# Graph layers on one Trainium2 core: one mixing matmul group per turn of 16 edge tiles in place of two of 8, with VectorE's one-hots made a turn ahead

## Chip, cores and metric

The kernel runs on 1 core of one Trainium2 chip. The metric is the device time of one execution in microseconds (us); less is better. An engine is named as the profile names it: PE is TensorE (PEld its weight loads), DVE is VectorE, ACT is ScalarE, POOL is GpSimd, SP is SyncE.

## What is computed

Four graph blocks run over 6,250 nodes with 128 features and one list of 106,250 edges, sorted by destination. Each block ends in a residual add and a layer norm. The blocks hold seven layers: five relational ones and two mean ones.

```python
# relational layer (three in block 0, two in block 2)
agg = segment_sum(h[src] @ W[etype], dst)        # 8 relations, W[r] is 128 x 128
h = relu(agg + h @ loopw + bias)  (+ h)
# mean layer (blocks 1 and 3)
agg = segment_sum(x[src] * weight, dst) / degree
x = concat(x, agg) @ W.T + b
```

The change touches the relational layers alone.

## The kernel before

**Tiles and turns.** The edges stand in 832 tiles of 128. The destinations of a tile lie in a window of 16 nodes, whose start is read at run time. A turn (`turn`, `messages`, `evacuate`) handles 16 tiles (`RING`), in two halves h of 8 (`HALF`), each half in two quarters q of 4 tiles. There are 52 turns in a layer (`TURNS`), so 260 in the five relational layers, which the trace shows from 18.7 to 1264 us, 1305 to 2596, 2629 to 3907, 4555 to 5824 and 5854 to 7120.

**What each engine does for one turn.**
- POOL (line 649) gathers the source rows of each tile from HBM by an indirect DMA, 8 per half, into `rows_in`. Before half h of a turn it waits for `summed[2h+1]` of the turn before (line 643), since the 8 places of that half are then free. Each place is written once a turn.
- DVE `onehots` (line 1300) makes the one-hot selectors of a quarter: 128 edges by 128 keys (16 nodes times 8 relations) for 4 tiles, as one instruction of 512 elements. It may overwrite them once `summed[2h+1]` has come.
- PE `messages` (line 1069) multiplies the gathered rows of a tile by its one-hot into a 128x128 piece of a PSUM bank, `SUM[q % 2]`, four tiles a bank. The last matmul of a quarter counts up `summed[q]`. It waits for the one-hots, for the four gathers one by one, and for the bank (`evacuated[(q + 2) % 4]`).
- ACT `evacuate_half` (line 777) copies the bank to `sums` in SBUF, sorted by relation, and counts up `evacuated[q]`. It waits for `summed[q]` and, ahead of each half, for `messaged[h]` of the turn before, since the mix has then read `sums`.
- PE (line 1082) mixes half h: 8 relations, each a 128x128 weight times 128 columns (8 tiles times 16 nodes), added up in its half of the PSUM bank `MIXED` (`MSG[h]`). The last one counts up `messaged[h]`. Ahead of the mix it waits for both evacuations of the half and for `added[7]` of the adds of that half's last use.
- DVE `adds` (line 1316) adds the 8 pieces of 128x16 to the columns of `acc` that their windows name, in order, each behind the one before by the semaphore `added[s]`.

A float32 matmul stands in the trace as two PE records, so a mix of a half is 16 records and a quarter of sums is 8.

**Order in a turn.** PE: sums of quarters 0 and 1, mix of half 0, sums of 2 and 3, mix of half 1. DVE (`turn`, line 1479): one-hots of half 1, adds of half 0, one-hots of half 0 of the turn that follows, adds of half 1. `opened` makes the one-hots of half 0 before the first turn. The engines' instruction streams are written out by hand in this order and each runs strictly in it.

**Fills.** In the four relational layers after the first, each half turn also builds four pieces of a dense adjacency matrix for the mean layers. DVE `hots` (lines 1396, 1400, 1405) makes markers into buffers of their own for each half, PE `fill` (line 955) multiplies them into two banks in turn, ACT `keep_fill` (line 748) copies them out and ACT's queue stores them by DMA (line 751). PE places the four fills of a half with `between`: two behind the sums of its quarters, one in the middle of its mix, one behind it. The fills are float32 in layers 1 and 2 and bfloat16 in layers 4 and 5.

**Steps between turns.** `edge_chunks` puts a step per chunk of 512 nodes between turns, once the adds for its nodes are done: DVE `columns` takes the chunk out of `acc`, PE turns it, ACT writes its rows to the table that the next layer gathers from. SP waits for `messaged` before each mean layer.

```python
pool.wait_ge(summed[2 * h + 1], k + (i + 1))                 # 643
pe.wait_ge(onehot_ready[q], this)                            # 1064
pe.wait_ge(evacuated[(q + 2) % 4], this)                     # 1065
pe.wait_ge(gathered[4 * q + t], landed)                      # 1067
pe.wait_ge(evacuated[2 * h + 1], following if h else this)   # 1077
pe.wait_ge(added[HALF - 1], taken[h])                        # 1078
act.wait_ge(messaged[h], k + 1)                              # 774
dve.wait_ge(summed[2 * h + 1], k + 1)                        # 1297
```

## Time and profile before

| what | us |
|---|---|
| runs shown | 7642.33, 7645.65, 7635.47 (median 7642.33) |
| the profiled execution | 7644.6 |
| its span in the profile | 7642.8 |
| busy: PE / PEld | 4968.5 / 4243.9 |
| busy: DVE / ACT / POOL | 3913.3 / 1543.1 / 3955.9 |
| idle before POOL's gathers from the tables | 2672.3 |
| granted share of PE's clock, mean | 0.797 |

The profiled execution's own time and its span differ by 1.8 us. Busy times are shares of an average over stages of different kinds: the five relational layers take some 6,350 us of the span, the rest are the two mean layers (3907 to 4555 and from 7120) and the short gaps between layers. Starts of PE instructions are recorded; their ends are modelled.

### The profile page before, as it was taken

Reading aid. Unit: us, or ns where it says so; the run is one execution under the profiler, and the core shown is the slowest. Engines: PE = TensorE matmul, PEld = TensorE weight load, DVE = VectorE, ACT = ScalarE, POOL = GpSimd, SP = SyncE. Lnnn points to the kernel's source line nnn. Section 1 sums busy time; section 2 is a strip of 40 time slices with the busy share of each in tenths; the row PEclk is TensorE's granted clock in tenths of the full one; section 3 lists DMA queues with packets and bytes.
Section 4 is the critical chain, followed back from the end, with each engine's and each line's share of the span. In section 5 each row is a group of like instructions: output and inputs, shape, how many; then the busy total and the mean of one; then the engine's idle time right before and its main releaser. Section 6 shows DMA issues by size and latency. Waiting matters only on the chain.

```text
span 7642.8 us, 106073 instructions
## 1 busy us (share of the span) xinstructions
PE 4968.5 (65%) x26408; PEld 4243.9 (56%) x26409; DVE 3913.3 (51%) x10762; ACT 1543.1 (20%) x3108; POOL 3955.9 (52%) x4190
## 2 busy tenths in 40 slices
PE   4444555667666667677679985555555555555799
PEld 4444444666666666666655545555554555555455
DVE  3222223555555555666666654444444454555666
ACT  1111111222222222222210012222222222222101
POOL 5666665566566566666630006666665666666100
PEclk7777766777878877878789997777777777777899
DMA  3122222344444334434458853333333333333464
GB/s 79 49 53 56 56 56 66 104 109 111 109 108 110 104 105 108 108 106 107 107 173 285 281 181 76 78 78 78 77 78 73 75 76 75 76 75 75 130 181 148
DMA packets 695057, 799.40 MB, mean 105 GB/s; under 512 B 307814, under 2 KB 582485, under 8 KB 694597
## 3 DMA queue, kind: packets, MB, share of 16 engines
q0 software_dynamic: 133952, 275.45, 17.5%
q10 hardware_dynamic: 481717, 270.72, 11.9%
q1 hardware_dynamic: 79184, 250.97, 10.1%
q8 instruction: 72, 1.18, 0.1%
q14 instruction: 132, 1.08, 0.0%
HBM read 529.43 MB, written 277.57 MB: 106 GB/s over the span
## 4 chain that ended last, share of the span: by engine, by line
PE 43%; another core or an unknown queue 28%; issue 15%; ACT 7%; ACTq 5%; DVE 2%; DMA 0%; DVEq 0%; SPq 0%
PE mixed L1082 17%; PE sum L986 6%; PE agg L955 5%; PE sum L1069 4%; ACT bulk L777 4%; PE fill L955 3%; ACT bulk L748 3%; PE mixed L986 3%; PE fill L986 3%; ACTq L751 2%; ACTq L161 1%; PE lin L930 1%; ACTq L154 1%; PE iota_ps L1112 1%
## 5 line engine op out<-in xcount | busy, mean ns | idle before, releaser
L649 POOL DMA_INDIRECT bulk<-h_table,srcT_i x3328 | 3151.9, 947 | 2672.3 <-remote 994.5
L1316 DVE TENSOR_TENSOR acc<-mixed,acc 128x16 f32 x4160 | 729.5, 175 | 2956.9 <-issue 1145.8
L1082 PE MATMUL mixed<-bulk,mix_w 128*128 128x128 f32 x4992 | 1092.2, 396 | 1277.7 <-ACT bulk L777 971.4
L1082 PEld LDWEIGHTS mixed<-bulk,mix_w 128*128 128x128 f32 x4992 | 1020.6, 300 | 1362.8 <-issue 1216.7
L1082 PE MATMUL mixed<-bulk,rel_w 128*128 128x128 f32 x3328 | 805.2, 420 | 1092.6 <-ACT bulk L777 1084.3
L1082 PEld LDWEIGHTS mixed<-bulk,rel_w 128*128 128x128 f32 x3328 | 722.6, 319 | 1143.3 <-issue 1138.2
L1069 PE MATMUL sum<-bulk 128*128 128x128 f32 x8320 | 1210.5, 295 | 23.8 <-issue 12.7
L1069 PEld LDWEIGHTS sum<-bulk 128*128 128x128 f32 x8320 | 1155.6, 213 | 35.0 <-issue 22.3
L777 ACT ACTIVATE bulk<-sum 128x512 f32<-128x512 f32 x1040 | 618.7, 598 | 2518.0 <-remote 1893.5
L649 POOL DMA_INDIRECT bulk<-in_x_dram,srcT_i x832 | 789.2, 949 | 482.0 <-issue 246.6
L1300 DVE TENSOR_TENSOR bulk<-iota_ps,keyT 128x512 f32<-128x512 f32 x1040 | 670.2, 686 | 210.6 <-issue 172.9
L1396 DVE TENSOR_TENSOR bulk<-iota_ps,low_key 128x392 bf16<-128x392 f32 (+1 forms) x1248 | 694.0, 556 | 5.1 <-issue 4.6
L748 ACT ACTIVATE bulk<-agg 128x392 f32<-128x392 f32 (+1 forms) x832 | 412.7, 496 | 1334.1 <-PE agg L955 835.6
L748 ACT ACTIVATE bulk<-fill 128x392 f32<-128x392 f32 (+1 forms) x832 | 417.8, 502 | 887.8 <-issue 355.6
L1400 DVE TENSOR_SCALAR bulk<-iota_ps,row_key,weight_of 128x128 f32<-128x128 f32 x1456 | 524.8, 402 | 1.8 <-issue 1.8
L986 PE MATMUL sum<-bulk,hT 128*128 128x448 f32 (+1 forms) x1176 | 434.9, 484 | 15.2 <-issue 7.8
L955 PE MATMUL agg<-bulk 128*128 128x196 f32 (+1 forms) x1664 | 419.7, 368 | 14.3 <-ACT bulk L748 8.0
L1432 DVE TENSOR_TENSOR bulk<-bulk 128x1792 f32<-128x1792 f32 (+1 forms) x192 | 344.1, 1792 | 103.3 <-DMA bulk<-adjacency_w 86.5
L955 PE MATMUL fill<-bulk 128*128 128x196 f32 (+1 forms) x1664 | 357.1, 322 | 27.9 <-issue 17.2
L1405 DVE TENSOR_TENSOR bulk<-iota_ps,row_key 128x256 bf16<-128x256 f32 x832 | 345.6, 415 | 3.9 <-issue 1.7
L955 PEld LDWEIGHTS agg<-bulk 128*128 128x128 f32 (+1 forms) x1664 | 292.7, 193 | 30.9 <-issue 14.6
L986 PEld LDWEIGHTS sum<-bulk,hT 128*128 128x128 f32 (+1 forms) x1176 | 187.1, 161 | 199.1 <-issue 163.8
(237 smaller groups left out, 3717.1 us busy)
## 6 DMA issues: line engine op xcount, KB each, us to landing
adjacency_w<-bulk ACTq DMA_DIRECT2D x416, 392.0 KB
bulk<-adjacency_w SPq DMA_DIRECT2D x147, 896.0 KB, 4.6
adjacency_n<-bulk ACTq DMA_DIRECT2D x416, 196.0 KB
bulk<-adjacency_n SPq DMA_DIRECT2D x147, 448.0 KB, 4.0
bulk<-h_table,srcT_i POOLq DMA_INDIRECT x3328
bulk<-adjacency_w SPq DMA_DIRECT2D x49, 448.0 KB, 4.1
bulk<-in_x_dram,srcT_i POOLq DMA_INDIRECT x832
h_table<-rows ACTq DMA_DIRECT2D x50, 256.0 KB
```

What stands on the lines that cost most here:

```text
L649: nc.gpsimd.indirect_dma_start(out=rows_in[:, s, :], out_offset=None, in_=rows_of[:, :], in_offset=bass.IndirectOffsetOnAxis(ap=srcT_i[:, ...
L748: act.activation(staged[m][s][:, f % 2 * 2 * LOWS:(f % 2 + 1) * 2 * LOWS], FILL[f % 2][:, 0:2 * LOWS], ACT.Copy).then_inc(fill_kept, 1)
L777: act.activation(sums[:, h, :, 4 * (q % 2):4 * (q % 2) + 4, :].rearrange("p r t v -> p t r v"), SUM[q % 2][:, :].rearrange("p (t r v) -> p ...
L955: last = nc.tensor.matmul(FILL[f % 2][:, w * LOWS:(w + 1) * LOWS], row[:, w, :], of[:, w, :], start=True, stop=True)
L986: last = nc.tensor.matmul(DENSE[s][:, 0:PIECE], x_k, (a_in, n_in)[m][t % bufs][:, s * PIECE:(s + 1) * PIECE], start=(n == 0 and k == 0), s ...
L1069: last = nc.tensor.matmul(SUM[q % 2][:, t * KEYS:(t + 1) * KEYS], rows_in[:, 4 * q + t, :], onehot[:, 4 * q + t, :], start=True, stop=True)
L1082: last = nc.tensor.matmul(MSG[h][:, 0:HALF * WIN], W[:, n, :], sums[:, h, n, :, :].rearrange("p t v -> p (t v)"), start=(n == 0), stop=(n ...
L1300: nc.vector.tensor_tensor(onehot[:, 4 * q:4 * q + 4, :], IOTA[:, 0:KEYS].unsqueeze(1).broadcast_to(each), keyT[:, bass.ds(i * RING + 4 * q ...
L1316: nc.vector.tensor_tensor(acc[:, at], MSG[h][:, s * WIN:(s + 1) * WIN], acc[:, at], ALU.add).then_inc(added[s], 1)
L1396: nc.vector.tensor_tensor(low_hots[f] if weighted else low_marks[f], IOTA[:, KEYS:NATURAL].unsqueeze(1).broadcast_to(each), low_key[:, bas ...
L1400: ins = nc.vector.tensor_scalar(row_hots[f][:, n, :], IOTA[:, NATURAL:NATURAL + D], row_key[:, bass.ds(w + n, 1)], weight_of[:, bass.ds(w ...
L1405: ins = nc.vector.tensor_tensor(row_marks[f], IOTA[:, NATURAL:NATURAL + D].unsqueeze(1).broadcast_to(each), row_key[:, bass.ds(w, 2)].unsq ...
```

## The change

Both halves of a turn are mixed by one group of 8 matmuls of 256 columns, behind the sums of all four quarters. `messaged` becomes one semaphore. PE waits once for evacuation (of quarter 3) and once for the adds of the turn before. DVE makes the one-hots of both halves of the following turn, and the fills' markers of both, and then adds all 16 pieces. `opened` makes both halves' one-hots. The fills of half 0 that stood in and behind its mix now stand between the sums of quarters 1 and 2; those of half 1 stand in and behind the one mix.

```diff
--- before.py
+++ after.py
@@ -379,7 +379,6 @@
 
         SUM = [bank("sum0"), bank("sum1")]
         MIXED = bank("mixed")
-        MSG = [MIXED[:, h * HALF * WIN:(h + 1) * HALF * WIN] for h in range(2)]
         LIN = [bank("lin0"), bank("lin1")]
         IOTA = bank("iota_ps")
         AGG = bank("agg")
@@ -402,7 +401,7 @@
         onehot_ready = [sem(f"onehot_ready{q}") for q in range(4)]
         summed = [sem(f"summed{q}") for q in range(4)]
         evacuated = [sem(f"evacuated{q}") for q in range(4)]
-        messaged = [sem(f"messaged{h}") for h in range(2)]
+        messaged = sem("messaged")
         added = [sem(f"added{s}") for s in range(HALF)]
         pass_moved = sem("pass_moved")
         waits_passed = sem("waits_passed")
@@ -547,9 +546,8 @@
                 m = layer["mean"]
                 if m == 0:
                     more_slices = slices_of(sp)
-                for h in range(2):
-                    sp.wait_ge(messaged[h], sp.snap(P * (REL_BEFORE[l] * TURNS) + 1))
-                    apart(sp)
+                sp.wait_ge(messaged, sp.snap(P * (REL_BEFORE[l] * TURNS) + 1))
+                apart(sp)
 
                 def restored():
                     if m == 0:
@@ -771,7 +769,8 @@
                         keep_lists(0)
 
                     def evacuate_half(h, k, between=None):
-                        act.wait_ge(messaged[h], k + 1)
+                        if h == 0:
+                            act.wait_ge(messaged, k + 1)
                         for q in (2 * h, 2 * h + 1):
                             act.wait_ge(summed[q], k + 1 + q % 2)
                             act.activation(
@@ -884,8 +883,7 @@
         def _(pe):
             for q in (1, 3):
                 pe.sem_inc(summed[q], 1)
-            for h in range(2):
-                pe.sem_inc(messaged[h], 1)
+            pe.sem_inc(messaged, 1)
             pe.sem_inc(filled, 8)
             pe.sem_inc(a_multiplied, A_BUFS)
             pe.sem_inc(degrees_turned, 1)
@@ -1059,7 +1057,7 @@
 
                         this, following = pe.snap(k + 1), pe.snap(k + 2)
                         landed = pe.snap(i * 16 + (GATHER_PASS * r + 16))
-                        taken = [pe.snap(k * 2 + (h + 2)) for h in range(2)]
+                        taken = pe.snap(k * 2 + 2)
                         for h in range(2):
                             for q in (2 * h, 2 * h + 1):
                                 pe.wait_ge(onehot_ready[q], this)
@@ -1071,20 +1069,23 @@
                                 last.then_inc(summed[q], 1)
                                 if between:
                                     between(h, q % 2)
-                            if h == 0 and layer["norm"] and c is not None and not (type(c) is int and c < 4):
-                                pe.wait_ge(x_kept, pe.snap(c + (NORM_BEFORE[l] * CHUNKS - 1)))
-                                apart(pe)
-                            pe.wait_ge(evacuated[2 * h + 1], following if h else this)
-                            pe.wait_ge(added[HALF - 1], taken[h])
-                            for n in range(N_RELS):
-                                if between and n == N_RELS // 2:
-                                    between(h, 2)
-                                last = nc.tensor.matmul(MSG[h][:, 0:HALF * WIN], W[:, n, :],
-                                                        sums[:, h, n, :, :].rearrange("p t v -> p (t v)"),
-                                                        start=(n == 0), stop=(n == N_RELS - 1))
-                            last.then_inc(messaged[h], 1)
-                            if between:
-                                between(h, 3)
+                            if between and h == 0:
+                                between(0, 2)
+                                between(0, 3)
+                        if layer["norm"] and c is not None and not (type(c) is int and c < 4):
+                            pe.wait_ge(x_kept, pe.snap(c + (NORM_BEFORE[l] * CHUNKS - 1)))
+                            apart(pe)
+                        pe.wait_ge(evacuated[3], following)
+                        pe.wait_ge(added[HALF - 1], taken)
+                        for n in range(N_RELS):
+                            if between and n == N_RELS // 2:
+                                between(1, 2)
+                            last = nc.tensor.matmul(MIXED[:, 0:RING * WIN], W[:, n, :],
+                                                    sums[:, :, n, :, :].rearrange("p h t v -> p h (t v)"),
+                                                    start=(n == 0), stop=(n == N_RELS - 1))
+                        last.then_inc(messaged, 1)
+                        if between:
+                            between(1, 3)
                 else:
                     pe.wait_ge(x_kept, 2 + CHUNKS * NORM_BEFORE[l])
                     pe.wait_ge(rows_ready, 4 + CHUNKS * l)
@@ -1301,20 +1302,21 @@
                                                 keyT[:, bass.ds(i * RING + 4 * q, 4)].unsqueeze(2).broadcast_to(each),
                                                 ALU.is_equal).then_inc(onehot_ready[q], 1)
 
-                def adds(h, i, k):
+                def adds(i, k):
                     _, starts = nc.values_load_multi_w_load_instructions(
-                        window[0:1, bass.ds(i * RING + HALF * h, HALF)], engines=[DVE], min_val=0, max_val=NP - WIN,
+                        window[0:1, bass.ds(i * RING, RING)], engines=[DVE], min_val=0, max_val=NP - WIN,
                         skip_runtime_bounds_check_because="starts are destinations, held to NP - WIN on the chip")
-                    earlier, this = dve.snap(k * 2 + (h + 2)), dve.snap(k * 2 + (h + 3))
-                    dve.wait_ge(messaged[h], k + 2)
-                    for s in range(HALF):
-                        if s:
-                            dve.wait_ge(added[s - 1], this)
+                    counts_of = [dve.snap(k * 2 + (h + 2)) for h in range(3)]
+                    dve.wait_ge(messaged, k + 2)
+                    for s in range(RING):
+                        h, place = s // HALF, s % HALF
+                        if place:
+                            dve.wait_ge(added[place - 1], counts_of[h + 1])
                         else:
-                            dve.wait_ge(added[HALF - 1], earlier)
+                            dve.wait_ge(added[HALF - 1], counts_of[h])
                         at = bass.ds(starts[s], WIN)
-                        nc.vector.tensor_tensor(acc[:, at], MSG[h][:, s * WIN:(s + 1) * WIN], acc[:, at],
-                                                ALU.add).then_inc(added[s], 1)
+                        nc.vector.tensor_tensor(acc[:, at], MIXED[:, s * WIN:(s + 1) * WIN], acc[:, at],
+                                                ALU.add).then_inc(added[place], 1)
 
                 def mark_steps():
 
@@ -1470,23 +1472,21 @@
 
                     def opened(p):
 
-                        onehots(0, 0, dve.snap(count(P, p, r, 0)))
-                        if layer["fills"] and p is more:
-                            fill_at(0, 0)
+                        for h in range(2):
+                            onehots(h, 0, dve.snap(count(P, p, r, 0)))
+                            if layer["fills"] and p is more:
+                                fill_at(0, h)
                         dve.wait_ge(acc_set, 2 + CHUNKS * (r + 1))
 
                     def turn(i, k, c=None, filling=False):
-                        onehots(1, i, k)
-                        if filling:
-                            fill_at(i, 1)
-                        adds(0, i, k)
                         with dve.If(i < TURNS - 1):
                             following = nc.s_assert_within(i + 1, min_val=1, max_val=TURNS - 1,
                                                            skip_runtime_bounds_check_because="the condition above")
-                            onehots(0, following, k + 1)
-                            if filling:
-                                fill_at(following, 0)
-                        adds(1, i, k)
+                            for h in range(2):
+                                onehots(h, following, k + 1)
+                                if filling:
+                                    fill_at(following, h)
+                        adds(i, k)
 
                     def turn_filling(i, k, c=None):
                         turn(i, k, c, True)
```

## Rows read from the trace of the kernel before

**Rows 1.** The page's parts 1 and 4: busy time, and the chain by engine.

```profile
PE 4968.5 (65%) x26408; PEld 4243.9 (56%) x26409; DVE 3913.3 (51%) x10762; ACT 1543.1 (20%) x3108; POOL 3955.9 (52%) x4190
...
PE 43%; another core or an unknown queue 28%; issue 15%; ACT 7%; ACTq 5%; DVE 2%; DMA 0%; DVEq 0%; SPq 0%
```

**Rows 2.** The five relational layers: length, busy PE, PEld, DVE, ACT, POOL, granted clock.

```profile
18.00:1264.00 1246.00, 618.00 (x3395) 581.69 (x3395) 303.05 (x1088) 140.77 (x241) 781.65 (x824) 0.73 0.22 55
1305.00:2595.00 1290.00, 878.56 (x4953) 844.02 (x4953) 747.49 (x2266) 309.50 (x642) 782.23 (x825) 0.79 0.40 107
2629.00:3907.00 1278.00, 896.07 (x4968) 847.13 (x4966) 773.90 (x2407) 308.94 (x646) 779.70 (x824) 0.80 0.40 106
4555.00:5824.00 1269.00, 706.75 (x4126) 656.75 (x4125) 611.50 (x1847) 326.11 (x641) 779.61 (x824) 0.76 0.36 77
5854.00:7119.00 1265.00, 707.53 (x4156) 655.70 (x4154) 636.69 (x1969) 325.75 (x647) 780.22 (x824) 0.77 0.36 75
```

**Rows 3.** Timeline, half a turn with float32 fills: start, busy us, instructions, idle before.

```profile
2112.09 0.60 ACT L777 ACTIVATE bulk<-sum 128x512 f32<-128x512 f32 x1 [2.46 <-remote]
...
2112.82 2.07 PE L1082 MATMUL mixed<-bulk,mix_w 128*128 128x128 f32 x8 [4.77 <-ACT bulk L777]
2112.86 0.95 POOL L649 DMA_INDIRECT bulk<-h_table,srcT_i  x1 [2.37 <-remote]
...
2114.68 1.51 PE L955 MATMUL agg<-bulk 128*128 128x196 f32 x4
...
2115.99 1.74 PE L1082 MATMUL mixed<-bulk,mix_w 128*128 128x128 f32 x8
...
2117.96 2.33 DVE L1316 TENSOR_TENSOR acc<-mixed,acc 128x16 f32 x8 [4.87 <-issue]
...
2118.23 1.05 PE L1069 MATMUL sum<-bulk 128*128 128x128 f32 x8
...
2119.78 1.05 PE L1069 MATMUL sum<-bulk 128*128 128x128 f32 x8
...
2121.62 0.95 POOL L649 DMA_INDIRECT bulk<-h_table,srcT_i  x1 [0.30 <-issue]
...
2124.29 0.60 ACT L777 ACTIVATE bulk<-sum 128x512 f32<-128x512 f32 x1 [5.35 <-remote]
...
2125.17 0.60 ACT L777 ACTIVATE bulk<-sum 128x512 f32<-128x512 f32 x1
2125.17 0.95 POOL L649 DMA_INDIRECT bulk<-h_table,srcT_i  x1 [2.60 <-remote]
```

**Rows 4.** Timeline, first layer, 16 gathers without a pause between the halves.

```profile
77.82 0.95 POOL L649 DMA_INDIRECT bulk<-in_x_dram,srcT_i  x1 [3.92 <-remote]
...
78.23 3.78 PE L1082 MATMUL mixed<-bulk,mix_w 128*128 128x128 f32 x16 [12.19 <-ACT bulk L777]
...
83.56 0.60 ACT L777 ACTIVATE bulk<-sum 128x512 f32<-128x512 f32 x1 [5.47 <-PE sum L1069]
...
86.06 0.60 ACT L777 ACTIVATE bulk<-sum 128x512 f32<-128x512 f32 x1 [1.90 <-remote]
...
87.82 0.94 POOL L649 DMA_INDIRECT bulk<-in_x_dram,srcT_i  x1 [0.30 <-issue]
...
90.14 1.95 PE L1069 MATMUL sum<-bulk 128*128 128x128 f32 x16
...
96.57 0.95 POOL L649 DMA_INDIRECT bulk<-in_x_dram,srcT_i  x1 [0.30 <-issue]
...
100.30 1.08 ACT L777 ACTIVATE bulk<-sum 128x512 f32<-128x512 f32 x2 [13.64 <-remote]
101.10 0.94 POOL L649 DMA_INDIRECT bulk<-in_x_dram,srcT_i  x1 [3.58 <-remote]
```

**Rows 5.** All instructions by line and shape: count, busy us, mean ns.

```profile
L1316 DVE TENSOR_TENSOR acc<-mixed,acc 128x16 f32 x4160 | 729.5, 175 | 2956.9 <-issue 1145.8 <-PE mixed L1082 943.3 <-remote 390.4
...
L1300 DVE TENSOR_TENSOR bulk<-iota_ps,keyT 128x512 f32<-128x512 f32 x1040 | 670.2, 686 | 210.6 <-issue 172.9 <-ACT weight_of L739 15.5 <-DVE window L1277 2.2
```

## The prediction

> **What bounds the kernel now.** I read the page first: PE is busy for 65% of the span, no engine for more, and 28% of the chain that ended last is time behind a releaser the profile can't name [rows 1]. So no engine is full, and a loop of waits is to be looked for. The five relational layers take 6,348 us of the span, and only they are changed. In them POOL issues 16 gathers a turn at the same pace whatever else is done: divided out (stretch / gathers x 16) a turn takes 24.2 us in the first layer and 25.1, 24.8, 24.6 and 24.6 in the others, although PE's busy time differs by 45% between them (618 to 896 us) and DVE's by 2.5 times [rows 2]. A loop whose length doesn't follow PE's or DVE's work is not set by them.
>
> The timeline of half a turn shows the loop [rows 3]. POOL starts its first gather at 2112.86 and its eighth at 2121.62, 8.76 us later (1.25 us each). The first of the next half starts at 2125.17, so 3.55 us behind the eighth, where 1.25 would be the pace: 2.3 us of pause. A half is thus 12.31 us, a turn 24.6. POOL waits there for the semaphore of the second quarter's sums. By the record those matmuls (those at 2119.78) were issued by 2120.8, but ACT, which waits for sums too, starts the copy of the first of these two quarters only at 2124.29 and of the second at 2125.17. So a semaphore of the sums is seen 3 to 5 us after its matmul, about when the gathers in flight can have landed; the mix's is seen at once (PE ends it near 2117.7, DVE adds from 2117.96). I can't say from these rows why. I take it as a fact: the sums' semaphores come late when PE reaches them late in a batch of eight gathers, and this delay, not PE's rate, makes the pause.
>
> The first layer shows the other case [rows 4]. There one quarter's copy starts at 83.56 and the other's at 86.06, before POOL has issued its batch out, and POOL goes from one half into the next without a pause (87.82 is 1.25 us behind its predecessor). The next release comes only behind the sixteenth gather (96.57): ACT at 100.30, POOL at 101.10. That turn took 101.10 - 77.82 = 23.28 us.
>
> **The change, part by part.**
>
> *The matmuls.* 16 records of 128 columns become 16 of 256 per turn instead of 32 of 128. The columns set this pace; the weight loads (PEld 844 us beside PE's 879 [rows 2]) lie under it. So a 256-column record should take twice as long and the mix saves nothing: 0 us. The bound on one side is half of the loads, if they did stand in the way: 4,160 fewer at 0.16 us (4243.9 / 26,409 [rows 1]), 670 us of PE's time, which would still not shorten a loop that PE doesn't set. The Trainium skill (Perfetto Trace Analysis, section Matmuls) says that larger matmuls are more efficient than smaller ones; by that rule PE's time would fall, by the rows above it stays, and the sum would be the same by both, since POOL's loop holds it.
>
> *One wait in place of two.* PE now issues all four quarters of sums of a turn, waits for the copy of quarter 3, mixes, and goes on with the sums of the next turn. Two things follow. The sums of quarters 2 and 3 stand directly behind the release of quarters 0 and 1, with no mix before them: copy 0.6 us, sums 1.0 to 1.7 us a quarter at either clock, so in the first layer they are out some 4 us after the release, in the layers with bfloat16 fills 5 to 6 us, with float32 fills 6 to 8 us. Today these sums stand behind 16 records of mix: in [rows 3] 6.9 us after PE's start. And a mix's semaphore, which today has that early place, is not held up. I take it that the semaphore of quarter 3 will then mostly be there when POOL has its eight gathers out (10.0 us), as at 86.06 in [rows 4], so POOL goes into the second half without a pause. The other half of the turn becomes heavier: a copy, a mix of 6.9 us at the lower level or 3.5 at the higher, two fills, the sums of quarters 0 and 1. Its release stays behind the last gather. A turn becomes that of [rows 4], 23.28 us.
>
> Price: 24.62 - 23.28 = 1.34 us a turn in four layers, x 208 = 279 us; in the first layer 24.2 - 23.28 = 0.9, x 52 = 47 us; 326 us in all. Bounds: 0 if the pause stays in both halves, 4.6 us a turn (24.6 - 20.0, 16 gathers at 1.25) if it goes from both. I take three quarters of 326, 245 us, nearest to the row of the same pattern, because in the float32 layers PE reaches quarter 3 late in a part of the turns.
>
> *DVE.* Adds and one-hots are as many as before: 16 x 0.29 = 4.7 us and 4 x 0.64 = 2.6 us a turn [rows 3, 5]. All DVE work of the heaviest layer is 774 us / 52 = 14.9 us a turn [rows 2], so 8 us and more are idle. New is that the adds are queued behind the one-hots and markers of both halves, and the markers of half 1 wait for fills that now stand in the mix. The adds will so come up to half a turn later. Who waits for them is PE's next mix, most of a turn on: cost 0, the idle 8 us are the cover; if that cover were gone, PE would wait, which is a rival below. The one-hots are made half a turn earlier than today or as early: 0.
>
> The Trainium skill (Perfetto Trace Analysis, section Matmuls) says that independent matmul groups should rotate through PSUM banks so that one's evacuation overlaps the next. This change goes the other way: before, the two halves had semaphores of their own; now one group can't start before all 16 adds of the last. By the rule that costs; no row of the kernel before has this wait.
>
> *ACT and POOL.* ACT's copies of quarters 0 and 1 wait for the one `messaged`, which is earlier in time than the sums they copy: 0. Fills: as many; ACT's copies of half 0's come closer together, and ACT is busy for a quarter of the time (309 of 1,290 us [rows 2]). POOL's gathers, its waits and its DMAs are the same. SP waits for `messaged` once instead of twice before two layers: 0, and its waits for `summed[3]` in the first layer only place background stores.
>
> *Ends of layers.* The last turn has nothing to hide the larger mix behind: 3.5 us more of mix, 8 x 0.29 = 2.3 us more of adds, and the first turn makes 1.3 us more of one-hots and, with fills, markers. About 6 us a layer, 30 us in all; bounds 0 and 60.
>
> **Sum.** 7644.6 (the profiled execution, 1.8 over its span, 2.3 above the median of the three runs) - 245 + 30 = 7429.6, and 2 less against the median: I say 7430.
>
> **Rivals.**
> *The loop stays locked* (chance 0.30). The pause remains in both halves, since the late semaphore is tied to the gathers in flight and not to PE's place. For it: the releases in [rows 3] come where the eighth gather can just have landed; in the layers with fills the delay is the same with heavy and with light work. Against: [rows 4]. Time: 7645 + 30 = 7675, between 7640 and 7700. I give 0.13 of it to within 0.2% and 0.17 to slower.
> *The heavy half becomes the bound* (0.17), slower. Place: from the release of quarter 3 to the last sum of the next turn's quarter 1, PE does a copy's wait of 0.7 us, 16 records of 256, three fills and 16 records of sums. At the lower level that is 0.7 + 6.9 + 3 x 1.4 + 3.4 = 15.2 us, at the higher about 8; allowed are 12.3 us less about 1, if the loop is locked. It decides from a mean of about 11 us on. Price: up to 3 us a turn in the 104 turns with float32 fills, 1 in the others: 100 to 400 us with the ends, 7,830 as a middle. For it: the granted clock is only 0.73 to 0.80 [rows 2]. Against: if the pause of one half goes, a turn leaves this chain over 20 us.
> *DVE's adds are exposed* (0.03): that rule's case. If the markers wait for the mix's fills and the adds behind them for PE, up to 4.7 us a turn would come onto the path, 7,800 to 8,800.
> *Both pauses go* (0.02): 20.0 us a turn, 7645 - 260 x 4.6 = 6,450.
> That the change doesn't do what it says has no place here: the instructions are counted in the diff; only its saving on PE is nil.
>
> **Numbers.** Forecast 0.48; its own range is 7,330 (all turns like [rows 4]) to 7,560 (a quarter of them). About 0.2% is what a measurement of this kernel can tell from no change (15 us). Faster: 0.48 + 0.02 = 0.50. Same: 0.13. Slower: 0.17 + 0.17 + 0.03 = 0.37. The range goes from 7,300 to 7,830: it leaves out half of the heavy-half case, the adds and the case of both pauses, and a little below.
>
> **What would show it.** In the changed kernel's timeline POOL's ninth gather of a turn 1.25 us behind its eighth, and one pause of 3 to 4 us a turn; 832 gathers in about 1,215 us in the float32 layers. `mixed` matmuls half as many, each twice as long, their busy time unchanged. DVE's adds in one run of 16. Wrong: two pauses a turn still (the locked loop); one pause much above 4 us, with PE busy up to the release (the heavy half); PE's idle time ahead of the mix put down to DVE's adds (the third). If PE's busy time in the mix falls by a third or more, my count of the weight loads is wrong.

## The result and the profile after

The changed kernel takes 7865.12 us (median of 3 runs, 7864.77 to 7875.04) against 7642.33: a ratio of 1.029, 95% interval 1.0275 to 1.0304. The forecast of 7430 us is wrong in sign, and the range of 7300 to 7830 does not hold the time. The profiled execution spans 7863.3 us, against 7642.8 before: 220.5 us are to be found.

The page of the changed kernel, parts 1 and 4, beside [rows 1]:

```profile
PE 4870.6 (62%) x22248; PEld 3787.7 (48%) x22249; DVE 3949.0 (50%) x10762; ACT 1538.1 (20%) x3108; POOL 3943.5 (50%) x4190
...
PE 36%; another core or an unknown queue 32%; issue 14%; ACT 6%; ACTq 4%; DVE 4%; POOL 2%; DMA 1%; DVEq 1%; POOLq 0%; SPq 0%
```

No engine is much busier than before (VectorE 36 us more, PE 98 and GpSimd 12 less); the share behind a releaser that the profile can't name rose from 28% to 32%. The five relational layers of the changed kernel (busy time by stretch, columns as in [rows 2]):

```profile
19.00:1244.00 1225.00, 632.22 (x2604) 508.85 (x2603) 304.57 (x1085) 141.21 (x243) 779.03 (x824) 0.67 0.22 56
1279.00:2582.00 1303.00, 832.63 (x4156) 736.79 (x4154) 768.66 (x2294) 321.63 (x653) 778.13 (x825) 0.83 0.39 106
2620.00:3973.00 1353.00, 839.97 (x4152) 742.80 (x4151) 784.44 (x2407) 320.64 (x647) 778.30 (x825) 0.82 0.37 100
4632.00:5944.00 1312.00, 696.20 (x3309) 566.68 (x3307) 617.05 (x1837) 315.15 (x642) 777.20 (x824) 0.71 0.33 74
5981.00:7327.00 1346.00, 707.46 (x3339) 577.56 (x3338) 643.40 (x1963) 317.05 (x646) 778.45 (x824) 0.71 0.32 70
```

Against [rows 2] the layers changed by -21, +13, +75, +43 and +81 us, 191 together; the other 29 us lie between the layers and behind the last, the term that the prediction called ends of layers and put at 30. They aren't the even 6 us a layer of the prediction: behind the five layers, in order, the changes are -6, +4, +11, +7 and +12 us (and +1 ahead of the first), so the agreement of the sum is in part luck. The table of waits by GpSimd (line, what it waited for: us in all, times, longest) says how, first of the kernel before:

```profile
POOL bulk L649 <- remote: 1200.5, 464, 4.2
...
POOL bulk L649 <- PE sum L1069: 106.5, 24, 16.1
```

and of the changed kernel:

```profile
POOL bulk L647 <- remote: 800.1, 316, 4.5
...
POOL bulk L647 <- PE sum L1067: 688.0, 110, 33.1
```

Of the half turns, 85, 103, 102, 101 and 102 began with a pause in the five layers before, and 51, 100, 96, 82 and 81 do now. But 110 of GpSimd's waits now last 6.3 us on average. To see which, I took for each turn the time from GpSimd's first gather to that of the next turn, 51 turns a layer:

| relational layer | turns up to 25.7 us, their mean | 25.7 to 28 us: number, us over 24.5 | over 28 us: number, us over 24.5 |
|---|---|---|---|
| before, 1 to 5 | 46 to 49; 23.60, 24.73, 24.75, 24.49, 24.50 | 3, 2, 2, 3, 2; 21 in all | 2, 1, 0, 0, 0; 20, 14, 0, 0, 0 |
| after, 1 | 49; 23.46 | 0 | 2; 17 |
| after, 2 | 47; 24.58 | 2; 5 | 2; 33 |
| after, 3 | 37; 24.53 | 6; 16 | 8; 74 |
| after, 4 | 23; 24.53 | 28; 52 | 0 |
| after, 5 | 28; 24.26 | 15; 28 | 8; 65 |

Three things stand in it: 16 very long turns in the third and fifth layer (139 us), turns of some 26.3 us, above all in the two bfloat16 layers (79 us more than before), and two turns of the second layer, mostly its first (19 us). What is left of the gain is the balance to 191, 46 us, of which 21 are the first layer's. The 19 us can't be put down to the change: one and the same kernel, run twice on one chip, showed that first turn at 50.5 us and at 33.3 (e10 and e16 below), where it is 52.9 here and 38.3 before.

**The first layer has the forecast pattern, but not its gain.** Timeline, one turn of the changed kernel:

```profile
703.84 0.95 POOL L647 DMA_INDIRECT bulk<-in_x_dram,srcT_i  x1 [0.30 <-issue]
...
713.84 0.94 POOL L647 DMA_INDIRECT bulk<-in_x_dram,srcT_i  x1 [0.30 <-issue]
717.64 1.09 ACT L776 ACTIVATE bulk<-sum 128x512 f32<-128x512 f32 x2 [18.28 <-remote]
...
718.47 0.94 POOL L647 DMA_INDIRECT bulk<-in_x_dram,srcT_i  x1 [3.69 <-remote]
```

The gathers left out start every 1.25 us, through the change of halves too (703.84 is the turn's eighth); from the start of the sixteenth gather to that of the next turn's first are 4.6 us (713.84 to 718.47), as in [rows 4]. The regular turns fell only from 23.60 to 23.46 us. By the starts of the gathers, the kernel before already had this pattern in 11 first-layer turns, at 23.66 us, beside 29 turns with both pauses, at 23.77: where the pause between the halves is missing, the one behind the sixteenth gather is longer (4.7 us in place of 3.0, from start to start).

**A very long turn.** Timeline of the changed kernel, third layer, where a chunk of nodes is finished:

```profile
3057.62 1.89 PE L1083 MATMUL mixed<-bulk,mix_w 128*128 128x256 f32 x8
...
3059.34 0.83 PE L953 MATMUL fill<-rel_w,bulk 128*128 128x196 f32 x4
...
3061.69 0.57 DVE L1398 TENSOR_TENSOR rel_w<-iota_ps,low_key 128x392 f32<-128x392 f32 x1 [2.56 <-PE fill L953]
3061.82 0.95 POOL L647 DMA_INDIRECT bulk<-h_table,srcT_i  x1 [0.30 <-issue]
...
3063.52 4.78 DVE L1318 TENSOR_TENSOR acc<-mixed,acc 128x16 f32 x16 [0.63 <-issue]
...
3068.45 1.09 PE L921 MATMUL mixed<-ident,rows 128*128 128x128 f32 x4 [7.84 <-DVE acc L1318]
...
3069.33 1.91 PE L1067 MATMUL sum<-bulk 128*128 128x128 f32 x8
...
3072.34 1.91 PE L1067 MATMUL sum<-bulk 128*128 128x128 f32 x8
...
3075.06 0.94 POOL L647 DMA_INDIRECT bulk<-h_table,srcT_i  x1 [12.30 <-PE sum L1067]
```

The same step of the kernel before:

```profile
3066.33 1.05 PE L1082 MATMUL mixed<-bulk,mix_w 128*128 128x128 f32 x8
...
3067.53 2.33 DVE L1316 TENSOR_TENSOR acc<-mixed,acc 128x16 f32 x8 [3.20 <-issue]
...
3070.01 0.63 PE L923 MATMUL mixed<-ident,rows 128*128 128x128 f32 x4 [1.52 <-issue]
...
3070.70 1.15 PE L1069 MATMUL sum<-bulk 128*128 128x128 f32 x8
3071.20 0.95 POOL L649 DMA_INDIRECT bulk<-h_table,srcT_i  x1 [0.30 <-issue]
...
3074.97 0.95 POOL L649 DMA_INDIRECT bulk<-h_table,srcT_i  x1 [2.82 <-PE sum L1069]
```

At the end of a chunk PE transposes normalised rows back (`back`, L921 after, L923 before) into the bank `mixed`, so it waits for every add out of that bank, and the next turn's sums stand behind it. Before, the last 8 adds start 0.15 us behind the mix, and `back` follows them 0.15 us on. After, VectorE has the next turn's markers of half 1 ahead of the adds; they wait for the fill behind the mix, so the adds start 4.0 us behind the mix (3059.51 to 3063.52), and there are 16 of them. GpSimd's pause, from start to start, is 13.24 us instead of 3.77. How long PE waited for VectorE's adds over the whole kernel (us in all, times, longest), ahead of the mix (L1082) and ahead of `back` (L923), before:

```profile
PE mixed L1082 <- DVE acc L1316: 118.5, 16, 12.0
...
PE mixed L923 <- DVE acc L1316: 12.3, 7, 2.0
```

and after, where the mix (L1083) has no such wait, with another wait that the change made:

```profile
PE agg L953 <- ACT bulk L746: 757.1, 203, 10.9
...
PE mixed L921 <- DVE acc L1318: 166.4, 19, 18.6
```

**A turn of 26 us.** The first of these lines (8.0 us, once, for the same wait before) is a second ring. Timeline of the changed kernel, fourth layer:

```profile
5210.92 0.44 PE L953 MATMUL agg<-bulk 128*128 128x196 bf16 x2
...
5213.55 1.06 PE L1067 MATMUL sum<-bulk 128*128 128x128 f32 x8
...
5216.12 0.94 POOL L647 DMA_INDIRECT bulk<-h_table,srcT_i  x1 [0.30 <-issue]
5219.43 0.50 ACT L746 ACTIVATE bulk<-agg 128x392 bf16<-128x392 f32 x1 [9.48 <-remote]
...
5220.07 0.48 PE L953 MATMUL agg<-bulk 128*128 128x196 bf16 x2 [5.46 <-ACT bulk L746]
5220.35 1.96 PE L1067 MATMUL sum<-bulk 128*128 128x128 f32 x8
...
5223.12 0.94 POOL L647 DMA_INDIRECT bulk<-h_table,srcT_i  x1 [6.05 <-PE sum L1067]
```

The fill in the mix is done at 5211.36, but ScalarE copies it out only at 5219.43, 3.3 us behind GpSimd's last gather. PE's first fill of the next turn needs that copy and stands between the sums of quarter 0 (5213.55) and quarter 1 (5220.35). GpSimd waits for quarter 1: 7.0 us from start to start in place of some 3.6.

### The profile page after: what moved, and what is told of

It reads as the page before. It is cut to its first block, busy times and chain, and to the rows that moved or that the text cites. A ratio compares the mean times of both kernels' runs of the same rounds, so it can differ in the third digit from the quotient of the medians.

```text
span 7863.3 us, 96647 instructions
## 1 busy us (share of the span) xinstructions
PE 4870.6 (62%) x22248; PEld 3787.7 (48%) x22249; DVE 3949.0 (50%) x10762; ACT 1538.1 (20%) x3108; POOL 3943.5 (50%) x4190
## 4 chain that ended last, share of the span: by engine, by line
PE 36%; another core or an unknown queue 32%; issue 14%; ACT 6%; ACTq 4%; DVE 4%; POOL 2%; DMA 1%; DVEq 1%; POOLq 0%; SPq 0%
PE mixed L1083 10%; PE sum L1067 6%; PE sum L984 6%; PE agg L953 4%; PE fill L953 3%; ACT bulk L746 3%; PE mixed L984 2%; PE fill L984 2%; ACT bulk L776 2%; ACTq L749 2%; POOL bulk L647 2%; DVE acc L1318 1%; ACTq L161 1%; DMA adjacency_n<-bulk 1%
## 5 line engine op out<-in xcount | busy, mean ns | idle before, releaser
L1067 PE MATMUL sum<-bulk 128*128 128x128 f32 x8320 | 1467.9, 331 | 546.3 <-ACT bulk L776 381.9
L1067 PEld LDWEIGHTS sum<-bulk 128*128 128x128 f32 x8320 | 1353.7, 241 | 608.8 <-issue 509.2
L1083 PE MATMUL mixed<-bulk,mix_w 128*128 128x256 f32 x2496 | 853.4, 506 | 653.4 <-ACT bulk L776 592.5
L1083 PEld LDWEIGHTS mixed<-bulk,mix_w 128*128 128x128 f32 x2496 | 634.1, 262 | 812.4 <-issue 697.8
L953 PE MATMUL agg<-bulk 128*128 128x196 f32 (+1 forms) x1664 | 394.9, 350 | 852.0 <-ACT bulk L746 757.1
L1083 PE MATMUL mixed<-bulk,rel_w 128*128 128x256 f32 x1664 | 598.1, 522 | 509.6 <-issue 314.8
L1083 PEld LDWEIGHTS mixed<-bulk,rel_w 128*128 128x128 f32 x1664 | 427.9, 271 | 614.2 <-issue 537.4
L953 PEld LDWEIGHTS agg<-bulk 128*128 128x128 f32 (+1 forms) x1664 | 238.5, 166 | 953.9 <-issue 934.7
L1398 DVE TENSOR_TENSOR rel_w<-iota_ps,low_key 128x392 f32<-128x392 f32 x416 | 233.4, 561 | 491.0 <-PE agg L953 151.0
L953 PE MATMUL fill<-bulk 128*128 128x196 f32 (+1 forms) x1664 | 379.4, 338 | 98.5 <-ACT bulk L746 59.6
```

The lines of the kernel that those rows point to most:

```text
L953: last = nc.tensor.matmul(FILL[f % 2][:, w * LOWS:(w + 1) * LOWS], row[:, w, :], of[:, w, :], start=True, stop=True)
L1067: last = nc.tensor.matmul(SUM[q % 2][:, t * KEYS:(t + 1) * KEYS], rows_in[:, 4 * q + t, :], onehot[:, 4 * q + t, :], start=True, stop=True)
L1083: last = nc.tensor.matmul(MIXED[:, 0:RING * WIN], W[:, n, :], sums[:, :, n, :, :].rearrange("p h t v -> p h (t v)"), start=(n == 0), stop= ...
L1398: nc.vector.tensor_tensor(low_hots[f] if weighted else low_marks[f], IOTA[:, KEYS:NATURAL].unsqueeze(1).broadcast_to(each), low_key[:, bas ...
```

## The experiments

Three theories were set against each other: the fill handshake just shown (T1), a heavy half in which the mix itself is too long (T2), and VectorE's new order (T3). An interval in brackets is 95%. Chips differ: the kernel before took 7648 us on the chip of e1 to e4, 7653 on that of e5 to e8, 7786 on that of e9 to e16, 7657 on the last. Each ratio is to the kernel before on the same chip. The drain at the chunks (T4) came up behind e1 to e4.

**e1**: PE's fills of half 0 behind quarter 1's sums.

```diff
-                                if between:
+                                if between and h:
                                     between(h, q % 2)
                             if between and h == 0:
-                                between(0, 2)
-                                between(0, 3)
+                                for f in range(4):
+                                    between(0, f)
```

> The changed kernel, with TensorE's four fills of half 0 issued behind the sums of quarter 1 instead of one of them between the sums of quarter 0 and quarter 1. The turns of the changed kernel take, layer by layer, 23.8, 25.3, 26.3, 25.5 and 26.1 us. Theory 1 (the fill handshake: this fill waits for ScalarE's copy of the last fill of the turn before, whose semaphore is seen only when the gathers in flight have landed, and the sums that GpSimd waits for stand behind it): the turns of the four layers with fills come towards the first layer's 23.8, 1.5 to 2.5 us less each, 208 turns, so 200 to 420 us less than 7865, 7450 to 7660. Theory 2 (the heavy half: TensorE has too much to do between quarter 3's release and quarter 1's sums, mostly the mix of 256 columns): only the one fill of 0.7 to 1.4 us leaves the way, at most 0 to 1 us a turn, 7650 to 7865, and TensorE is busy up to quarter 1's sums. Theory 3 (VectorE's adds or one-hots are late since they moved): no change, 7850 to 7880.

7712.8 us, 1.0083 (1.0065 to 1.0101). About 150 us less than the changed kernel: above T1's range, and inside the one I had given T2. What tells them apart is where it went. The turns of 25.7 to 28 us are all but gone (1 of 51 in the fourth layer, 0 in the fifth), and GpSimd's waits for sums fell by half:

```profile
POOL bulk L647 <- PE sum L1067: 307.6, 48, 30.5
```

The 16 turns over 28 us stayed (64 and 58 us over 24.5, from 74 and 65), and the two float32 layers still pause twice a turn, which T1 had not reckoned with. By T2 the 26 us turns would have lost the one fill of at most 1.4 us, and PE would be busy up to quarter 1's sums; they lost 1.8 us, and what stood there was a wait.

**e2**: both halves' fills behind both quarters' sums, ScalarE's copies of sums ahead of those of fills.

```diff
...
-                                if between:
-                                    between(h, q % 2)
-                            if between and h == 0:
-                                between(0, 2)
-                                between(0, 3)
+                            if between:
+                                for f in range(2 if h else 4):
+                                    between(h, f)
```

> The changed kernel, with the fills of each half behind the sums of both its quarters on TensorE, and ScalarE's copies of both quarters ahead of its copies of fills. Theory 1 (the fill handshake): no quarter's sums and no quarter's copy stand behind a fill now, so the layers with fills come at least as near to the first layer's 23.8 us a turn as with half 0 alone: 7430 to 7640. Theory 2 (heavy half, the mix's length): 7650 to 7865. Theory 3 (VectorE): 7850 to 7880.

7720.5 us, 1.0093 (1.0075 to 1.0111): nothing beyond e1, and again above T1's range.

**e3**: one mix, VectorE's order of before.

```diff
...
                     def turn(i, k, c=None, filling=False):
+                        onehots(1, i, k)
+                        if filling:
+                            fill_at(i, 1)
                         with dve.If(i < TURNS - 1):
...
-                            for h in range(2):
-                                onehots(h, following, k + 1)
-                                if filling:
-                                    fill_at(following, h)
+                            onehots(0, following, k + 1)
+                            if filling:
+                                fill_at(following, 0)
                         adds(i, k)
```

> The changed kernel with VectorE's order of one-hots and markers of before: those of half 1 at the start of the turn, those of the next turn's half 0 ahead of the adds; the one mix of 16 tiles and the one run of 16 adds stay. It undoes the part of the change that is VectorE's alone. Theory 3 (the new order on VectorE is what costs): towards the time before, 7640 to 7750. Theories 1 and 2 (the way runs through TensorE and ScalarE, VectorE's part costs nothing): 7840 to 7900, the light half's and the heavy half's lengths as in the changed kernel; a slower time than that would say that making one-hots a turn ahead helps.

7732.7 us, 1.0097 (1.0075 to 1.0119): T3's range, which I had counted as the weakest. The long turns shrink from 74 and 65 us over 24.5 to 42 and 36, the turns of 25.7 to 28 us from 100 us over 24.5 to 48 (with no fill moved), and what PE waited for adds ahead of `back` from 166.4 us to:

```profile
PE mixed L921 <- DVE acc L1318: 76.4, 13, 13.8
```

**e4**: e2's order of fills and copies in the kernel before.

```diff
...
                                 last.then_inc(summed[q], 1)
-                                if between:
-                                    between(h, q % 2)
+                            if between:
+                                for f in range(2):
+                                    between(h, f)
```

> The kernel before, with the fills of each half behind the sums of both its quarters (TensorE), and ScalarE's copies of both quarters ahead of its copies of fills. In the kernel before the turns are 24.2 us without fills and 24.6 to 25.0 with them. Theory 1 (the handshake costs only where a fill stands ahead of sums that are on the way): the layers with fills come to 24.2 or below, 0.4 to 0.9 us x 208 turns, 80 to 190 us less, 7450 to 7560. Theory 2 (TensorE's amount of work per half sets the half): the amount is the same, so 7620 to 7660. If the fills' new place makes the mix late instead: slower than 7660.

7618.1 us, 0.9959 (0.9944 to 0.9973): faster by 30 us, where T1 said 80 to 190. The fills' place costs little as long as two mixes leave no fill's copy on the way.

**e5 and e6**: `back` writes to `sum0`, in the changed kernel and in e1's. PE's wait for `x_kept`, ScalarE's copy of what `back` wrote, moves with it from ahead of the mix to the start of the turn.

```diff
-        BACK = {REL: MIXED, MEAN: AGG}
+        BACK = {REL: SUM[0], MEAN: AGG}
...
-                    pe.wait_ge(added[HALF - 1], pe.snap(taken))
+                    pe.wait_ge(evacuated[2], pe.snap(taken))
```

> The changed kernel, with the transposes back of a finished chunk (PE's function back) written to the bank sum0 in place of the bank mixed, so that they wait for ScalarE's copy of quarter 2 and no longer for the 16 adds out of mixed. In the changed kernel eight turns of the third relational layer take 33 to 34 us where their neighbours take 24.5, and eight of the fifth 29 to 35; each of them follows the end of a chunk, where PE waits for all adds before it transposes back, and the next sums stand behind it. Theory 4 (these turns are the drain: one mix and 16 adds must end before the bank is free): they fall to about the neighbours, 16 turns x 6 to 9 us, and some turns behind them with 27.5 too, 100 to 180 us less than 7865: 7690 to 7765. Rival (the drain comes from the chunk's other work, columns and normalising behind the adds on VectorE): 7830 to 7880.

> The changed kernel with both remedies: the four fills of half 0 behind the sums of quarter 1, and the transposes back in the bank sum0. The first alone measured 7713. If the handshake of the fills and the drain at the chunks are separate costs, both gains add: 7713 less 90 to 160, 7550 to 7625, below the kernel before (7642). If they are one cost seen twice: 7690 to 7720.

e5: 7847.6 us, 1.0242 (1.0225 to 1.026); e6: 7687.3 us, 1.0037 (1.0023 to 1.0051). Both miss, e5 by far; e6 comes out 3 us under its second range. The wait mostly moved. `back` now runs at once (3045.46 in e6), but the next sums need ScalarE's copy out of `sum0`, and ScalarE stands behind the late fill. Timeline of e6:

```profile
3045.46 0.60 PE L921 MATMUL sum<-ident,rows 128*128 128x128 f32 x4
...
3047.27 0.50 ACT L746 ACTIVATE bulk<-fill 128x392 f32<-128x392 f32 x1 [3.94 <-remote]
...
3051.27 0.58 ACT L707 ACTIVATE xT<-sum 128x512 f32 x1
...
3052.35 3.78 PE L1070 MATMUL sum<-bulk 128*128 128x128 f32 x16 [6.29 <-ACT xT L707]
```

So the bank alone is not the cause. It has a part in it: e6 lies below e1 (1.0037 against 1.0083, on two chips), and its long turns hold 91 us over 24.5 where e1's hold 123.

**e7 and e8**: GpSimd waits quarter by quarter, in the kernel before and in e4's.

```diff
-                        for h in range(2):
-                            pool.wait_ge(summed[2 * h + 1], k + (i + 1))
+                        for q in range(4):
+                            pool.wait_ge(summed[q], k + (i + 1))
...
```

> The kernel before, with GpSimd waiting for the sums quarter by quarter (summed 0 ahead of four gathers, summed 1 ahead of the next four) instead of for the second quarter of a half ahead of all eight. Theory A (the semaphores of both quarters' sums come at about the landing of the last gather in flight, the first some 0.9 us ahead of the second): each half starts up to 0.9 us earlier, 520 halves, of which I count a half to all: 230 to 450 us less, 7190 to 7410. Theory B (TensorE's chain of sums and mix sets the period and the pause only shows it): the gathers start earlier and wait later, 7620 to 7660.

> The kernel before with the waits of GpSimd quarter by quarter and the fills of a half behind both quarters' sums (the two edits of e4 and e7 together). In e4 the fills' new place alone measured 0.996 of before. Theory A: both gains, 7160 to 7390, as the first quarter's semaphore comes at the landing but the second's now has no fill ahead of it. Theory B: 7600 to 7640, as e4.

7666.4 us, 1.0018 (1.0007 to 1.0029), and 7670.4 us, 1.0022 (1.0011 to 1.0034): theory A falls, as a forecast of the time, and for e8 even theory B was too good. The trace of e7 shows more than its time. Its regular turns are shorter in the four layers with fills (24.46, 24.63, 24.20 and 24.22 us, before 24.73, 24.75, 24.49 and 24.50), but nine turns in the third and fifth layers now take some 30 us and hold 49 us over 24.5. An earlier start of four gathers buys a little in every turn, and as much is lost in these, with two mixes and VectorE's order of before.

**e9**: one mix in the first and fourth relational layer alone, two elsewhere, on e4's base.

```diff
+        ONE_MIX = (0, 4)
...
+                        one = l in ONE_MIX
                         for h in range(2):
...
+                            if one:
+                                continue
                             if h == 0 and layer["norm"] and c is not None
...
+                        if one:
...
+                                last = nc.tensor.matmul(MIXED[:, 0:RING * WIN], W[:, n, :],
```

> The one mix of 16 tiles, with VectorE's order and adds of the change, in the first and the fourth relational layer only (those that have no chunks to normalise and, by their gathers, gained or can gain: 1,225 against 1,246 us in the first, 1,248 against 1,268 in the fourth once the fills stand behind the sums); the other three keep two mixes of 8 tiles. Fills stand behind both quarters' sums everywhere, as in e4 (7618). If the mix's cost is the handshake of the fills and the drain at the chunks, neither of which these two layers now have: 7618 less 20 to 45, 7570 to 7600, the first kernel here clearly below the one before. If a mix of 16 costs by itself (TensorE's heavy half): 7620 to 7680.

7756.9 us, 0.9962 (0.9948 to 0.9976), on a chip on which the kernel before is slower; as a gain over e4 (0.9959 elsewhere) it shows none. By layer it is less clear. Against e12, which has the instructions of the kernel before on this chip, the two layers with one mix are 24 and 15 us shorter (1241.3 and 1268.6 us from the first gather to the last half's; 1265.5 and 1284.0), and the third layer, with two mixes, is 14 longer: seven of its turns take some 32 us, where e12 has four. Whether the new place of the fills makes these, no run on this chip shows.

**e10 and e16**: e1 and e3 together. It was run twice, both times on the slow chip, although the text of e16 speaks of another.

> The changed kernel with the fills of half 0 behind the sums of quarter 1 (e1, 7713) and with VectorE's order of before (e3, 7733); only the one mix and the one run of 16 adds are left of the change. If both edits remove the same wait (the fills' handshake; VectorE's markers for half 1's fills are a link of it): 7690 to 7720, no better than the better one. If they remove different ones (the fills on TensorE's way, VectorE's queue ahead of the adds at the chunks): the gains add in part, 7610 to 7680.

> The same kernel as e10: one mix, fills of half 0 behind quarter 1's sums, VectorE's order of before. Measured on another chip: 0.994. If the two remedies add: 0.990 to 1.003 and at least 0.005 below e14. If the gain was that chip's: as e14, 1.005 to 1.012.

7738.1 us, 0.9937 (0.992 to 0.9953), and 7731.3 us, 0.9931 (0.9913 to 0.9949). The first was expected as a time of the faster chips, and is comparable only as a ratio: there it is below e1 and e3, though on another chip.

**e11 and e15**: VectorE's order alone, two mixes. It too was run twice, both times on the slow chip, so e15 can't tell whether the cost is that chip's. The markers of half 1 stand between the two runs of adds, since PE's second mix needs the first run.

```diff
-                        onehots(1, i, k)
-                        if filling:
-                            fill_at(i, 1)
-                        adds(0, i, k)
                         with dve.If(i < TURNS - 1):
...
                                 fill_at(following, 0)
+                            onehots(1, following, k + 1)
+                        adds(0, i, k)
+                        with dve.If(i < TURNS - 1):
...
+                            if filling:
+                                fill_at(following, 1)
                         adds(1, i, k)
```

> The kernel before with two mixes of 8 tiles, and VectorE's one-hots of both halves made a turn ahead of their use, as in the change; the markers of half 1 stand between the two runs of 8 adds, as far ahead as two mixes allow. It does the change's VectorE part alone. If the new order costs by itself: 7700 to 7780, as e3 gave back 130 us. If it costs only with one mix, whose 16 adds stand behind it: 7635 to 7665. If one-hots made early help: below 7635.

> The same kernel as e11: two mixes, VectorE's one-hots of both halves a turn ahead. Measured on another chip: 1.021. Theory V (the order is the larger cost because the adds stand behind one-hots that wait for the sums of the running turn): 1.015 to 1.025 again. If the first result was that chip's: 1.00 to 1.01.

7950.2 us, 1.0207 (1.0187 to 1.0227), and 7950.4 us, 1.0214 (1.0196 to 1.0232). With e13 and e14 on the same chip the change comes apart:

> The changed kernel as it is, beside e14, e15 and e16 on one chip, since times of one kernel differ by some 2% between chips. Measured first: 1.029 of before. Expected 1.015 to 1.035.

> The same kernel as e3: the one mix and the run of 16 adds, VectorE's one-hots and markers in the order of before. With e11 (VectorE's order alone) and the changed kernel this makes the four combinations. Measured as e3: 1.010. If VectorE's order is the larger cost, this stays at 1.00 to 1.012, and e15 above it; if the one mix is the larger, this lies above 1.015.

| same chip | ratio | us over 24.5 in turns over 28, layers 3 and 5 |
|---|---|---|
| one mix alone (e14) | 0.9969 (0.9956 to 0.9982) | 42, 29 |
| VectorE's order alone (e15) | 1.0214 (1.0196 to 1.0232) | 75, 68 |
| both, the change (e13) | 1.0113 (1.0095 to 1.0131) | 82, 65 |
| one mix, fills behind sums (e16) | 0.9931 (0.9913 to 0.9949) | 38, 20 |

VectorE's order by itself is worse than the whole change and makes the same long turns. Its 165 us are not its price in the change, though. With two mixes it also puts the adds of half 0 behind one-hots that wait for quarter 3's sums, which with one mix stand ahead of the adds anyway. In the change the order costs 113 us on this chip (e13 less e14). Timeline of e15, the end of a chunk:

```profile
3162.04 0.57 DVE L1396 TENSOR_TENSOR rel_w<-iota_ps,low_key 128x392 f32<-128x392 f32 x1 [3.20 <-remote]
...
3163.25 2.33 DVE L1316 TENSOR_TENSOR acc<-mixed,acc 128x16 f32 x8
...
3165.73 1.08 PE L923 MATMUL mixed<-ident,rows 128*128 128x128 f32 x4 [5.01 <-DVE acc L1316]
...
3171.74 0.94 POOL L649 DMA_INDIRECT bulk<-h_table,srcT_i  x1 [11.74 <-PE sum L1069]
```

The same chain as in the changed kernel, with two mixes: a marker that waits, adds behind it, `back` behind them. Its other turns in the layers with fills are longer too, 25.0 to 25.3 us, but only a little: e12, the instructions of before on this chip, has 24.9 to 25.1. e13 and e14 came out lower than I had written; the one mix alone is a small gain on this chip and a loss of 1% on that of e3, and e16 lies 0.4% below it, not the 0.5% asked for, though by both its runs below the kernel before. The fills' place is worth less here because the 26 us turns are nearly absent: in e13, the changed kernel itself, the turns of 25.7 to 28 us hold 36 us over 24.5, in e12 29, where they hold 100 and 21 in the first profiles of the two kernels. Yet PE's fills wait for ScalarE about as often and as long in e13 as in the first profile (300 times, 738 us, against 288 times, 817 us), so that row alone doesn't tell what the ring costs.

**e12**: sums of the identity matrix instead of the gathered rows.

```diff
-                                    last = nc.tensor.matmul(SUM[q % 2][:, t * KEYS:(t + 1) * KEYS], rows_in[:, 4 * q + t, :],
+                                    last = nc.tensor.matmul(SUM[q % 2][:, t * KEYS:(t + 1) * KEYS], ident[:, :],
```

> The kernel before, with the sums taken of the identity matrix in place of the gathered rows; TensorE still waits for each gather. It leaves out the messages' data, nothing of the instructions. If TensorE's sums are seen late because it reads the memory that the gathers write to: the pause of 3.6 us a half goes or shrinks, 6500 to 7400. If the lateness is one of the semaphores and the gathers in flight: 7630 to 7660, same pauses.

Measured once: 7795.2 us against 7785.8 before on that chip, with the pauses as they were (2.90 us):

```profile
2173.77 0.94 POOL L649 DMA_INDIRECT bulk<-h_table,srcT_i  x1 [0.31 <-issue]
2177.61 0.94 POOL L649 DMA_INDIRECT bulk<-h_table,srcT_i  x1 [2.90 <-remote]
```

That PE reads what the gathers write is not why its semaphores are late.

**e17**: e16 with the 16 adds ahead of the next turn's markers of half 0; **e18**: the kernel before.

```diff
                             onehots(0, following, k + 1)
-                            if filling:
-                                fill_at(following, 0)
                         adds(i, k)
+                        if filling:
...
+                                fill_at(following, 0)
```

> The kernel of e10 and e16 (one mix, the fills of half 0 behind quarter 1's sums, VectorE's order of before) with one more edit: VectorE's run of 16 adds stands ahead of the next turn's markers of half 0, not behind them. Sixteen turns behind the ends of chunks still take 28 to 30 us in e16 where their neighbours take 24.8, about 60 us in all. If VectorE's queue (markers that wait for fills, adds behind them) makes these turns long: 30 to 60 us less than e16, 0.985 to 0.990 of before where e16 was 0.993. If it is ScalarE's and TensorE's work at the chunk: as e16, within 10 us. If markers made later hold up the fills: slower than e16.

> The kernel before itself, for its profile on a second chip, as its times differ between the chips (about 7650 and 7785) while those of the changed kernel don't (7865 and 7871). If the difference sits in the turns at the ends of chunks: eight turns of the third relational layer at 31 to 33 us on the slower chip, as in e12's trace, none on the faster. If it sits in every turn: 24.9 to 25.1 us instead of 24.5 to 24.8, with the landing of a gather 0.2 us later. On the same chip as the first time: as before, 7633 to 7655.

e17 takes 7716.3 us, 1.0082 (1.0061 to 1.0103), and its long turns are still 27 to 35 us: a miss. These markers were not the rest of the drain. Whether e16 itself would be faster than before on this chip is open: it was run on the slow one alone, and e17 differs from it by chip and edit at once. Its time is 15 us below e16's, its ratio 1.5% above. e18 is the kernel before (0.9988) on a chip like the first. There it has two such long turns in the third layer (16 us over 24.5) and none in the fifth; e12, the same instructions on the slow chip, has four there (34 us), not the eight of e18's text. So the kernel before has some of these long turns too. That a chip's timing decides how many is argued, not shown: GpSimd's idle time behind the eighth gather is 2.9 us there (median, e12) and 2.7 here. No run profiles the kernel before itself, with the gathered rows, on the slow chip.

## Why the prediction was wrong

From the forecast to the time are 435 us: 199 of gain that did not come, 139 for the long turns at the ends of chunks, 79 for the turns of 26 us and 19 in the second layer, mostly its first turn.

**The first release without a pause** (the gain of 245 us): right in place in the first layer, far too large in size. The first layer gave 21 of the 47 us counted at full; the five layers together 46. The term mis-sized is the price of a pause, 1.34 us a turn, which set a turn of one layer against turns of others. In one layer, turns without the second pause are shorter than those with it by 0.1 us in the kernel before (first layer, 23.66 against 23.77), and by 0.6 and 0.8 us in the bfloat16 layers of e1: what one pause loses, the other takes up in part. The 24.2 us for the first layer was a stretch divided out, and two turns of 35 and 33 us were in it; its regular turns took 23.60 already, 0.3 above [rows 4]. The step "I take it that the semaphore of quarter 3 will then mostly be there when POOL has its eight gathers out" held in one layer and failed in the two with float32 fills, which still pause in 100 and 96 of 103 half turns (103 and 102 before); in the bfloat16 layers it held in about a fifth (82 and 81 pauses, 101 and 102 before). Timeline of the changed kernel, second layer:

```profile
2131.05 1.05 PE L1067 MATMUL sum<-bulk 128*128 128x128 f32 x8
...
2135.91 0.94 POOL L647 DMA_INDIRECT bulk<-h_table,srcT_i  x1 [0.30 <-issue]
...
2138.64 0.60 ACT L776 ACTIVATE bulk<-sum 128x512 f32<-128x512 f32 x1 [1.01 <-remote]
...
2139.41 0.94 POOL L647 DMA_INDIRECT bulk<-h_table,srcT_i  x1 [2.56 <-remote]
```

PE reaches quarter 3 almost 5 us ahead of the eighth gather, as I had worked out, and its semaphore comes behind that gather all the same. I had generalised from a layer without fills ([rows 4]) to layers with them. That is the locked loop (0.30) for these layers; its price of 30 us for the ends of layers is what was measured in all (29), with a different split.

**The adds queued behind one-hots and markers, "cost 0"**: the largest cost that the sum put at nothing. I wrote that the adds come up to half a turn later and that only PE's next mix waits for them. `back` waits for them as well, and so does VectorE's own reading of a finished chunk; both stand in the loop at every end of a chunk, sixteen times in two layers, at 5 to 11 us each. The rival had the right mechanism, markers that wait for the fills in the mix and the adds behind them, but I charged it to every turn, gave it 7,800 to 8,800 and a chance of 0.03. The time fell in that interval at its low end. Without VectorE's new order the change takes 132 us less than where it was first timed (e3, 1.0097 in place of 1.029) and 113 us less on the slow chip (e14, 0.9969 in place of 1.0113). Only on the slow chip does that turn the sign. On chips like the first every kernel with one mix in all layers is slower than the kernel before, by 0.4 to 2.9%: the gain that should have carried the change was too small to pay for anything. And the order is not the whole of the long turns. Of the 139 us in them, e3 keeps 79; the one mix with its 16 adds makes these by itself (e14: 71 us, e12 34).

The rule of the Trainium skill (Perfetto Trace Analysis, section Matmuls), that matmul groups should rotate through PSUM banks, was set aside because "no row of the kernel before has this wait". That reading was wrong: PE's mix waited for the adds 16 times before, 118.5 us in all, 15 of them in the first layer; one of 9.8 us ends at 101.9, just behind the turn of [rows 4]. After the change the mix has none of these waits, so what the prediction feared did not happen at the mix. The wait shows ahead of `back`, the bank's other writer, at 166.4 us, so the trace agrees that a shared bank is where a wait shows; e5 and e6, with the bank changed, won little of it.

**"Fills: as many; copies come closer together", 0**: wrong. The fill in the mix is copied late, and the first fill of the next turn stood between quarters 0 and 1. It is 79 us in the table. e1 leaves 6 of the 100 us that these turns hold, and e3, with no fill moved, leaves 48, so VectorE's order feeds this ring as well, and the gains of e1 and e3 don't simply add.

**The heavy half** (0.17) named the right half and the right sign, near the right time, for the wrong reason: PE was not busy up to the release, it stood for 5.46 us on ScalarE's copy. e1, which shortens no mix, shows that.

**The mix saves nothing on PE**: nearly right. Its busy time fell from 1897.4 us (1092.2 + 805.2) to 1451.5:

```profile
L1083 PE MATMUL mixed<-bulk,mix_w 128*128 128x256 f32 x2496 | 853.4, 506 | 653.4 <-ACT bulk L776 592.5
...
L1083 PE MATMUL mixed<-bulk,rel_w 128*128 128x256 f32 x1664 | 598.1, 522 | 509.6 <-issue 314.8
```

Eight records of 256 columns take 3.77 us at 1.2 GHz and 1.89 at 2.4 (granted clock 0.50 and 1.00 in the two parts of the mix at 3053 and 3057.6), sixteen of 128 take 3.78 us at 1.2 GHz in [rows 4]: the same columns, the same time. In the trace the records of 128 columns start 0.213 us apart at 1.2 GHz, those of 256 columns 0.427, just twice. So a column costs the same, as the prediction had it, although its division there is off (3.78 / 16 is 0.236, not 0.21; the difference is the modelled end of the last record, once in a group). The rule of the Trainium skill (Perfetto Trace Analysis, section Matmuls) that larger matmuls are more efficient shows in no row here. Two things made the busy time fall. There are 468 such ends in place of 936, which I estimate at some 130 us from these rows (0.36 us each at the lower level, half that at the higher). And the clock is higher: 84% of the steps between the mix's records were at the lower level before, 48% after, some 320 us by the same estimate. No run shows any of it in the time: the kernel whose mix was busy for 446 us less took 220 us more.

## What to carry to other kernels

When a consumer is queued behind work for a later turn, list every waiter of its results, those at block boundaries first: one that comes sixteen times in a kernel can cost more than all the regular turns give (139 us against 46). Price a pause by turns with it and without it in one and the same stage, since another pause can grow when it goes. Test the parts of a change one by one on the same chip; here VectorE's order, which costs on both chips where it was taken out, was sold together with one mix, which alone gained 0.3% on one chip and lost 1% on another. A pattern read in a stage without some side work (fills) is not evidence for the stages that have it.
